# Spectral block on one core: three banks for the inverse column transform, a fifth layer 1 eviction on ScalarE, the second LN2 product behind layer 1

## Chip, cores and metric

The kernel runs on one core of a Trainium2 chip. The time is device time of one execution in microseconds (us), median of 3 executions; all data are float32.

## What is computed

Input x is (16, 56, 56, 64): 16 images of 56 x 56 pixels with 64 channels. Two layers follow each other.

```python
# layer 0: whitening over all pixels
f = x_flat - mean                                   # 64 x 50176
ff = (1 - EPS) * (f @ f.T) / (n - 1) + EPS * eye
f_hat = solve_triangular(cholesky(ff), eye) @ f     # then * gamma + beta
# layer 1: Fourier filter block and MLP, per image
h = layer_norm(x, n1_g, n1_b)
xf = rfft2(h)                                       # 56 x 29 frequencies, 8 blocks of 8 channels
o1 = relu(complex 8x8 products of xf with w1, + b1) # filter layer 1
o2 = softshrink(complex products of o1 with w2, + b2, 0.01)   # filter layer 2
h = irfft2(o2) + h + x
out = gelu(layer_norm(h, n2_g, n2_b) @ mw1 + mb1) @ mw2 + mb2 + h
```

## The kernel before

The 16 images go in 8 pairs; a pair is a tile of 112 rows (2 images x 56 image rows) and 56 x 64 columns. First comes the covariance of all pairs and its factorization (up to about 124 us), which gives the whitening matrix `wy`. Then the pairs run as a software pipeline written out by hand: each engine has its own instruction list, and they meet only at semaphores.

Step i (the `step` function of TensorE, ScalarE and VectorE) works on pair i, and besides on the pair before and the two after. TensorE does in order: `dft_h` (S1, transform along the columns, 8 chunks, line 1020), a whitening chunk of pair i+1 (line 1005), `dft_w` (S2, line 1030), a whitening chunk, `layer_1` (line 1045, four groups of two chunks), a whitening chunk, then seven slices of the MLP of pair i-1. Slice 0 begins with the transposes of `n2` (line 1106) and whitening chunks 3 to 6; slices 1 and 2 hold `layer_2` (line 1061), slices 3 and 4 `inv_w` (INVW, line 1072), slices 5 and 6 `inv_h` (FIN, line 1093, four pairs of chunks: the inverse column transform). In each slice come the MLP's two products (`mlp_in`, line 1115, and `mlp_out`, line 1124) and the transposes back (`turn_out`, line 1133). In slices 1 to 3 x of pair i+2 is transposed as well (line 990) for steps up to 5.

PSUM has eight banks. Bank 0 (`BANK_X`) takes x chunks and whitening chunks 0 to 4; banks 1 and 2 take the chunks of pair i from L2 on, in turn (`B_BANK`), and whitening chunks 5 and 6; bank 3 (`BANK_M`) the MLP's transposes and second product and its turned output; banks 4 to 7 the MLP's hidden values, and parts of S1, S2 and L1. A chunk's product waits until the chunk that had its bank before has been read; `free_b` and `free_c` issue that wait.

Evictions are split by kind. ScalarE reads S1, S2, INVW, the x chunks, `n2T` (line 1307), gelu (line 1314) and `mlp_t` (line 1323), and of the eight chunks of L1 those not in `L1_DVE` (line 1292, two instructions each). VectorE reads the others of L1 (line 680, two each), L2 (line 691, then a clamp from SBUF to SBUF, line 697), FIN (line 719), the whitening chunks (line 671) and the MLP's output slice (line 706). It also does the statistics (line 587) and the normalizations; `multiply_rstd` (line 632) is the product of LN2 for half of a pair. GpSimd does, for each pair, two long operations on the residual (`add_h`, lines 416 and 419), which wait for both products of the pair before (`n2_ready`), and then the difference that makes the softshrink, chunk by chunk (line 429), which gives `y_ready`. Chunk c of L2 has the buffer of chunk c-2, so VectorE's eviction waits for `y_ready` of that one. SyncE issues all transfers.

Of the kernel before, what the change touches and what calls it, by code (L numbers as in the profile page):

```python
# [35 lines left out]
PAIRS = B // 2  # L36
# [15 lines left out]
S1, S2, L1, L2, INVW, FIN, B_CHUNKS = 0, 8, 16, 24, 32, 40, 48  # L52
A_CHUNKS = 14
BANK_X, BANK_M, BANK_HID = 0, 3, 4
# [6 lines left out]
def last_pair(i):  # L61
    return i == PAIRS - 1


L1_DVE = (1, 3, 5, 7)
B_READERS = [("act",)] * B_CHUNKS
for _k in range(8):
    B_READERS[L2 + _k] = ("dve",)
    B_READERS[FIN + _k] = ("dve",)
for _k in L1_DVE:  # L70
    B_READERS[L1 + _k] = ("dve",)


def b_done(who, k):

    return sum(who in readers for readers in B_READERS[:k + 1])


B_ACT, B_DVE = (b_done(who, B_CHUNKS - 1) for who in ("act", "dve"))
# [23 lines left out]
B_BANK = [(1, 2, 4, 5, 6, 7)[k % 6] if k < L2 else 1 + k % 2 for k in range(B_CHUNKS)]  # L103
# [9 lines left out]

def fin_bank(i, k):

    return BANK_HID + k - 2 if i == 0 and 2 <= k < 6 else B_BANK[FIN + k]


def mlp_order(i):
# [55 lines left out]
def build(nc, x, consts, params, out):  # L175
# [5 lines left out]
    with ExitStack() as ctx:  # L181
# [3 lines left out]
        def sem(name):  # L185
            return ctx.enter_context(nc.semaphore(name))
# [7 lines left out]
        def pp(name, rows=128):  # L194
            return prm[0:rows, p_at[name][0]:p_at[name][1]]
# [84 lines left out]
        a_act, whitened = sem("a_act"), sem("whitened")  # L280
        b_act, b_dve = sem("b_act"), sem("b_dve")
# [10 lines left out]
        bank = [psum[:, j, :] for j in range(8)]  # L292
# [21 lines left out]
        def bc(ap2, n):  # L314

            return ap2.unsqueeze(2).broadcast_to((ROWS, n, C))
# [21 lines left out]
        with nc.Block() as block:  # L338
# [110 lines left out]
            def _(dve):  # L449
# [115 lines left out]
                def folded_weights():  # L565

                    dve.wait_ge(s_mlp_ps, 2)
                    nc.vector.tensor_tensor(hbias[:], hb_ps, pp("mb1"), ALU.add).then_inc(s_mlp, 1)
                    nc.vector.scalar_tensor_tensor(mw1s[:], mwm_ps, -float(ROWS) / C, mw1s[:], ALU.mult, ALU.add).then_inc(s_mlp, 1)
# [55 lines left out]
                def half_w(t, k):  # L625
                    return t[:, k * WP * C:(k + 1) * WP * C].rearrange("p (w c) -> p w c", c=C)

                def multiply_rstd(i, k):

                    if i == 0 and k == 0:  # L630
                        dve.wait_ge(r_begun, 3)
                    nc.vector.tensor_tensor(half_w(n2, k), half_w(rf[i % 2], k), bc(small[:, 8, k * WP:(k + 1) * WP], WP),  # L632
                                            ALU.mult).then_inc(n2_ready, 1)
# [24 lines left out]
                def ln2(i):  # L658
                    mean_rstd(i, 1)
                    if i < PAIRS - 2:  # L660
                        ev_whiten(i + 2, [0])
                    for k in range(2):
                        multiply_rstd(i, k)

                def ev_whiten(i, ks):
                    if i > 1:

                        dve.wait_ge(r_begun, 2 * i - 1)
                    for k in ks:
                        dve.wait_ge(pe_a, i * A_CHUNKS + 7 + k + 1)  # L670
                        nc.vector.tensor_tensor(  # L671
                            y_of(i)[:, k * 512:(k + 1) * 512].rearrange("p (w c) -> p w c", c=C),
                            bank[(WHITEN if i > 1 else SECOND_WHITEN)[k]][0:ROWS, :].rearrange("p (w c) -> p w c", c=C),
                            row("beta", 8), ALU.add).then_inc(whitened, 1)

                def ev_layer_1(i):
                    for k in L1_DVE:
                        dve.wait_ge(pe_b, i * B_CHUNKS + L1 + k + 1)
# [50 lines left out]
                def step(i, ahead, behind):  # L729
                    def slice_(s, e0, e1, e2, e3):  # L730

                        e0()
                        e1()
                        e2()
                        if behind and s > 0:
                            ev_mlp(i - 1, s - 1)
                        e3()

                    def next_(what, *args):
                        if ahead:  # L740
                            what(i + 1, *args)

                    def whitened_next(*ks):
                        if i > 0:
                            next_(ev_whiten, ks)
# [14 lines left out]
                    ev_layer_1(i)  # L760
                    if i == 0:
                        folded_weights()
                    slice_(0, lambda: whitened_next(2, 3, 4), lambda: whitened_next(5),
                           lambda: whitened_next(6), lambda: stats_next(0))
                    slice_(1, lambda: ev_layer_2(i, [0]), lambda: (ev_layer_2(i, [1]), stats_next(1)),
# [63 lines left out]
            def _(pe):  # L829
# [245 lines left out]

                def free_fin(i, k):

                    if i > 0 or k < 2:
                        return free_b(i, FIN + k)
                    if k >= 6:  # L1080
                        pe.wait_ge(b_dve, b_done("dve", FIN + k - 6))
                    return bank[fin_bank(i, k)]

                def inv_h(i, k):
# [163 lines left out]
            def _(act):  # L1248
# [38 lines left out]
                def ev_layer_1(i):  # L1287
                    for k in range(8):
                        if k not in L1_DVE:
                            act.wait_ge(pe_b, i * B_CHUNKS + L1 + k + 1)  # L1290
# [259 lines left out]
```

## Time and profile before

| | |
|---|---|
| median of 3 executions | 806.96 us (805.65 to 807.21) |
| the profiled execution | 809.76 us |
| its span | 808.0 us |
| busy: TensorE matmul, weight load | 765.6 us (95%), 531.2 us (66%) |
| busy: VectorE, ScalarE, GpSimd | 561.5 us (69%), 393.7 us (49%), 263.1 us (33%) |
| steps 2 to 5, each | 82.9 us |
| step 6, step 7 with what follows | 81.56 us, 122.75 us |

Busy shares are means over stages. The steps begin at 141.07 (step 0), 191.59, 272.19, 355.06, 437.94 (step 4), 520.82, 603.69 (step 6) and 685.25 us (step 7). Where the prediction reads a single step, it is step 4 unless it says otherwise. In the rows, line numbers are those of the kernel before; in brackets stands how long an engine was idle before the row and who released it.

### The profile page before, as it was taken

How to read it: one execution, taken by the hardware profiler on the slowest of the kernel's cores; microseconds unless marked ns; L12 is line 12 of the kernel's file. 1: busy time of each engine (PE TensorE's matmuls, PEld its weight loads, DVE VectorE, ACT ScalarE, POOL GpSimd, SP SyncE). 2: the span in 40 equal slices, each digit the busy share in tenths (PEclk: the TensorE clock that was granted, in tenths of full speed). 3: DMA queues.
4: the chain of work that ended last, by engine and by line, in shares of the span. 5: the costliest groups of instructions: out<-in, count | busy, mean ns of one | idle time of the engine just before them, and what ended most of it. 6: DMA issues, size and time to landing. Idle time of an engine off the chain costs nothing.

```text
span 808.0 us, 18673 instructions
## 1 busy us (share of the span) xinstructions
PE 765.6 (95%) x7561; PEld 531.2 (66%) x7561; DVE 561.5 (69%) x1860; ACT 393.7 (49%) x757; POOL 263.1 (33%) x107
## 2 busy tenths in 40 slices
PE   7998998998999999999999999999999999989887
PEld 5994558886666676657765777486748665747333
DVE  4568988799777677767685858585958695733651
ACT  0011006743756374736563656475646544755365
POOL 5000000953740364035412551245223622362000
PEclk9899999999999999999999999999999999999999
DMA  9934002011000210112010300130000000000012
GB/s 273 277 97 144 3 2 81 1 48 35 1 25 24 74 41 14 35 46 70 13 35 24 92 13 24 35 92 13 24 30 18 12 25 24 24 12 24 24 35 69
DMA packets 10375, 39.50 MB, mean 49 GB/s; under 512 B 1282, under 2 KB 1410, under 8 KB 8834
## 3 DMA queue, kind: packets, MB, share of 16 engines
q1 hardware_dynamic: 10290, 38.31, 16.4%
q8 instruction: 60, 0.98, 0.5%
q14 instruction: 25, 0.20, 0.1%
HBM read 25.46 MB, written 12.85 MB: 47 GB/s over the span
## 4 chain that ended last, share of the span: by engine, by line
PE 84%; DVE 12%; issue 2%; ACT 1%; DMA 0%; DVEq 0%; ACTq 0%
PE psum L1115 11%; PE psum L1124 11%; PE psum L1020 7%; PE psum L1061 7%; PE psum L1030 6%; PE psum L1072 6%; PE psum L1045 6%; PE psum L1093 5%; PE psum L1005 4%; PE psum L844 4%; PE psum L895 3%; PE psum L1133 3%; PE psum L990 3%; DVE stats L587 2%; PE psum L1106 2%
## 5 line engine op out<-in xcount | busy, mean ns | idle before, releaser
L1314 ACT ACTIVATE hid<-psum,hbias 128x448 f32<-128x448 f32 x224 | 123.8, 635 | 80.6 <-PE psum L1115 80.6
L411 POOL TENSOR_TENSOR rbuf<-ybuf,prm 112x2560 f32<-112x2560 f32 (+2 forms) x7 | 31.8, 4539 | 224.8 <-DVE hbuf L816 130.4
L1115 PE MATMUL psum<-n2T,mw1s 64*128 64x448 f32 x448 | 102.7, 576 | 1.7 <-ACT n2T L1307 1.7
L429 POOL TENSOR_TENSOR p_y<-layer,clamped 128x512 f32<-128x512 f32 x64 | 75.6, 1181 | 80.1 <-DVE clamped L697 80.1
L1124 PE MATMUL psum<-hid,prm 128*64 128x448 f32 x448 | 96.3, 552 | 1.9 <-DVE oslice L706 1.9
L691 DVE TENSOR_TENSOR layer<-psum,prm 128x512 f32<-128x512 f32 x64 | 40.3, 630 | 42.8 <-PE psum L1061 42.8
L1061 PEld LDWEIGHTS psum<-w2s,o_g 128*64 128x64 f32 x1856 | 60.1, 138 | 14.4 <-issue 8.9
L416 POOL TENSOR_TENSOR hbuf<-hbuf,prm 112x3584 f32<-112x3584 f32 x8 | 49.6, 6204 | 59.9 <-DVE n L632 59.9
L1072 PEld LDWEIGHTS psum<-cst,p_y 128*128 128x128 f32 x512 | 61.2, 192 | 10.6 <-issue 6.3
L1072 PE MATMUL psum<-cst,p_y 128*128 128x112 f32 x512 | 66.8, 277 | 0.5 <-DVE layer L691 0.5
L1061 PE MATMUL psum<-w2s,o_g 128*64 128x64 f32 x1856 | 66.1, 224 | 0.9 <-ACT o_g L1292 0.6
L1124 PEld LDWEIGHTS psum<-hid,prm 128*64 128x64 f32 x448 | 27.3, 136 | 58.4 <-issue 42.8
L1093 PE MATMUL psum<-u_r,cst 58*112 58x448 f32 x256 | 55.2, 551 | 8.3 <-DVE rbuf L719 4.1
L1115 PEld LDWEIGHTS psum<-n2T,mw1s 64*128 64x128 f32 x448 | 39.9, 189 | 30.0 <-issue 21.6
L1005 PE MATMUL psum<-wy,xT 128*112 128x128 f32 x448 | 57.1, 277 | 1.9 <-DVE ybuf L671 1.2
L1005 PEld LDWEIGHTS psum<-wy,xT 128*112 128x112 f32 x448 | 51.3, 177 | 10.9 <-issue 10.0
L1020 PEld LDWEIGHTS psum<-cst,hbuf 112*112 112x112 f32 x512 | 52.3, 177 | 9.2 <-issue 8.5
L1020 PE MATMUL psum<-cst,hbuf 112*112 112x116 f32 x512 | 55.1, 265 | 2.8 <-DVE rbuf L719 1.6
L1261 ACT COPY u_r<-psum 112x464 f32<-112x464 f32 x64 | 34.9, 545 | 45.7 <-PE psum L1020 45.7
L411 POOL TENSOR_TENSOR fbuf<-ybuf,prm 112x2560 f32<-112x2560 f32 (+1 forms) x6 | 24.4, 4075 | 93.8 <-DVE oslice L706 93.8
L1030 PE MATMUL psum<-cst,u_r 112*128 112x116 f32 x464 | 53.4, 276 | 1.3 <-ACT u_r L1261 1.3
L587 DVE BATCH_NORM_STATS2 stats<-ybuf 112x6 f32<-112x64 f32 x392 | 52.9, 207 | 1.8 <-ACT ybuf L1397 1.6
(135 smaller groups left out, 1382.3 us busy)
## 6 DMA issues: line engine op xcount, KB each, us to landing
xin<-x_dram SPq DMA_DIRECT2D x8, 1568.0 KB, 8.3
out_dram<-oslice SPq DMA_DIRECT2D x56, 224.0 KB, 2.2
ybuf<-x_dram SPq DMA_DIRECT2D x2, 1568.0 KB, 15.9
fbuf<-x_dram SPq DMA_DIRECT2D x2, 1568.0 KB, 19.1
xin<-x_dram SPq DMA_DIRECT2D x4, 392.0 KB, 4.9
n<-x_dram SPq DMA_DIRECT2D x1, 1568.0 KB, 21.3
n<-x_dram SPq DMA_DIRECT2D x4, 392.0 KB, 13.2
prm<-params_dram SPq DMA_DIRECT2D x1, 742.0 KB, 4.2
```

The source lines that it names most:

```text
L411: nc.gpsimd.tensor_tensor(r3, y3, row("b1", ws.stop - ws.start), ALU.add).then_inc(r_begun, 1)
L429: nc.gpsimd.tensor_tensor(yk, a, b, ALU.subtract).then_inc(y_ready, 1)
L587: last = nc.vector.bn_stats(stats[:, w, :], src[:, w * C:(w + 1) * C])
L1005: last = nc.tensor.matmul(t[0:ROWS, j * 128:(j + 1) * 128], xT[:, w * ROWS:(w + 1) * ROWS], wy[:], start=(i > 0), stop=True, skip_group_ch ...
L1020: last = nc.tensor.matmul(t[0:ROWS, j * 2 * KR:(j + 1) * 2 * KR], h_w[:, 4 * k + j, :], cc("f1", ROWS), start=True, stop=True)
L1030: last = nc.tensor.matmul(t[:, j * 4 * KF:(j + 1) * 4 * KF], u_r[0:ROWS, (4 * k + j) * 128:(4 * k + j + 1) * 128], cc("f2", ROWS), start=T ...
L1061: last = nc.tensor.matmul(t[C * r:C * r + C, j * C:j * C + C], o_g[:, at:at + C], w2s[:, 128 * half + C * r:128 * half + C * r + C], start ...
L1072: last = nc.tensor.matmul(t[:, j * 112:j * 112 + 112], y_v[:, 4 * k + j, :], cc("invw"), start=True, stop=True)
L1093: one = nc.tensor.matmul(t[d][0:ROWS, 0:7 * C], cc("invh")[rows, ROWS * m:ROWS * m + ROWS], g[rows], start=(m == 0), stop=(m == 1))
L1115: nc.tensor.matmul(t[:, 0:4 * ROWS], mw1s[C * v:C * v + C, HH * m:HH * m + HH], n2T[C * v:C * v + C, s % 2, :], start=True, stop=True).the ...
L1124: last = nc.tensor.matmul(t[C * v:C * v + C, 0:4 * ROWS], pp("mw2")[:, C * m:C * m + C], hid[:, s % 2, m, v, :], start=(m == 0), stop=(m = ...
L1314: nc.scalar.activation(hid[:, s % 2, m, v, :], bank[CH_MLP[i].bank[k]][:, 0:4 * ROWS], ACT.Gelu, bias=hbias[:, m:m + 1]).then_inc(c_act, 1)
```

## The change

Three edits. In steps 1 to 6 the chunks of the inverse column transform take banks 1, 2 and 0 in turn instead of 1 and 2, so that a chunk waits for the one three before it; chunk 2, the first in bank 0, waits for the last x chunk's eviction (for the last whitening chunk's in step 6). Chunk 1 of L1 goes from VectorE to ScalarE in all eight steps, which then has 0, 1, 2, 4 and 6. And VectorE does the second product of LN2 after its evictions of L1 instead of right after the first.

```diff
-L1_DVE = (1, 3, 5, 7)
+L1_DVE = (3, 5, 7)
...
 def fin_bank(i, k):
 
-    return BANK_HID + k - 2 if i == 0 and 2 <= k < 6 else B_BANK[FIN + k]
+    if i == 0 and 2 <= k < 6:
+        return BANK_HID + k - 2
+    return (1, 2, BANK_X)[k % 3] if 0 < i < PAIRS - 1 else B_BANK[FIN + k]
...
                     if i < PAIRS - 2:
                         ev_whiten(i + 2, [0])
-                    for k in range(2):
-                        multiply_rstd(i, k)
+                    multiply_rstd(i, 0)
...
                     ev_layer_1(i)
                     if i == 0:
                         folded_weights()
+                    if behind:
+                        multiply_rstd(i - 1, 1)
                     slice_(0, lambda: whitened_next(2, 3, 4), lambda: whitened_next(5),
...
                 def free_fin(i, k):
 
-                    if i > 0 or k < 2:
+                    if k < 2 or last_pair(i):
                         return free_b(i, FIN + k)
-                    if k >= 6:
-                        pe.wait_ge(b_dve, b_done("dve", FIN + k - 6))
+                    if i == 0:
+                        if k >= 6:
+                            pe.wait_ge(b_dve, b_done("dve", FIN + k - 6))
+                        return bank[fin_bank(i, k)]
+                    if k == 2 and i < PAIRS - 2:
+                        pe.wait_ge(a_act, (i + 3) * 7)
+                    elif k == 2:
+                        pe.wait_ge(whitened, (i + 2) * 7)
+                    else:
+                        pe.wait_ge(b_dve, i * B_DVE + b_done("dve", FIN + k - 3))
                     return bank[fin_bank(i, k)]
```

VectorE around layer 1 of step 1, before (`n` is the buffer `n2`, the output of the LN2 product; `o_g` the output of layer 1):

```order
L632 TENSOR_TENSOR n<-rbuf,small 112x1792 [waits r_begun]
L632 TENSOR_TENSOR n<-rbuf,small 112x1792
L671 TENSOR_TENSOR ybuf<-psum,prm 112x512 [waits pe_a,r_begun]
L680 TENSOR_SCALAR o_g<-psum,prm 64x15x29 [waits pe_b]
L680 TENSOR_SCALAR o_g<-psum,prm 64x15x29
L680 TENSOR_SCALAR o_g<-psum,prm 64x15x29 [waits pe_b]
L680 TENSOR_SCALAR o_g<-psum,prm 64x15x29
L680 TENSOR_SCALAR o_g<-psum,prm 64x14x29 [waits pe_b]
L680 TENSOR_SCALAR o_g<-psum,prm 64x14x29
L680 TENSOR_SCALAR o_g<-psum,prm 64x14x29 [waits pe_b]
L680 TENSOR_SCALAR o_g<-psum,prm 64x14x29
L671 TENSOR_TENSOR ybuf<-psum,prm 112x512 [waits pe_a,r_begun]
```

The same place with the change (lines 634, 672 and 681 are the former 632, 671 and 680):

```order
L634 TENSOR_TENSOR n<-rbuf,small 112x1792 [waits r_begun]
L672 TENSOR_TENSOR ybuf<-psum,prm 112x512 [waits pe_a,r_begun]
L681 TENSOR_SCALAR o_g<-psum,prm 64x15x29 [waits pe_b]
L681 TENSOR_SCALAR o_g<-psum,prm 64x15x29
L681 TENSOR_SCALAR o_g<-psum,prm 64x14x29 [waits pe_b]
L681 TENSOR_SCALAR o_g<-psum,prm 64x14x29
L681 TENSOR_SCALAR o_g<-psum,prm 64x14x29 [waits pe_b]
L681 TENSOR_SCALAR o_g<-psum,prm 64x14x29
L634 TENSOR_TENSOR n<-rbuf,small 112x1792
L672 TENSOR_TENSOR ybuf<-psum,prm 112x512 [waits pe_a,r_begun]
```

One eviction of two instructions has left the queue, and the second product now stands behind the rest of them and ahead of the whitening chunks 2 to 6.

TensorE at the inverse column transform of step 1, before (`u_r` holds the spectrum that `inv_h` reads):

```order
L1093 MATMUL psum<-u_r,cst 112x448 [waits b_act]
L1093 MATMUL psum<-u_r,cst 112x448 x3
L1106 MATMUL psum<-cst,n 128x112 [waits c_act]
L1106 MATMUL psum<-cst,n 128x112 x3
L1093 MATMUL psum<-u_r,cst 112x448 [waits b_dve,b_act]
L1093 MATMUL psum<-u_r,cst 112x448 x3
```

And with the change:

```order
L1104 MATMUL psum<-u_r,cst 112x448 [waits b_act]
L1104 MATMUL psum<-u_r,cst 112x448 x3
L1117 MATMUL psum<-cst,n 128x112 [waits c_act]
L1117 MATMUL psum<-cst,n 128x112 x3
L1104 MATMUL psum<-u_r,cst 112x448 [waits b_dve,a_act,b_act]
L1104 MATMUL psum<-u_r,cst 112x448 x3
```

The order is the same; the second pair of chunks waits in addition for the x chunks' evictions (`a_act`), and `b_dve` there stands for one eviction fewer.

## Rows read from the trace of the kernel before

**Rows 1.** Page, part 4: the chain that ended last, shares of the span

```profile
PE 84%; DVE 12%; issue 2%; ACT 1%; DMA 0%; DVEq 0%; ACTq 0%
```

**Rows 2.** Stretches: length, busy PE, PEld, DVE, ACT, POOL, PEclk, DMA, GB/s

```profile
437.94:520.82 82.88, 81.18 (x735) 56.45 (x735) 59.38 (x195) 47.39 (x91) 31.66 (x12) 1.00 0.14 40
707.40:710.00 2.60, 0.59 (x5) 0.41 (x5) 1.27 (x2) 1.69 (x3) 2.46 (x2) 1.00 0.00 0
710.00:713.40 3.40, 3.40 (x9) 1.43 (x9) 0.00 (x0) 1.19 (x3) 3.40 (x1) 0.50 0.00 0
```

**Rows 3.** Waits of PE in step 4: total us, times, longest

```profile
PE psum L1093 <- DVE rbuf L719: 0.9, 1, 0.9
```

**Rows 4.** Timeline, PE behind layer 1 of step 4: start us, duration us

```profile
454.97 5.92 PE L1045 MATMUL psum<-p_y,w1s 64*128 64x435 f32 x32
...
462.36 0.57 PE L1106 MATMUL psum<-cst,n 112*128 112x112 f32 x4 [0.41 <-ACT o_g L1292]
463.13 1.10 PE L1005 MATMUL psum<-wy,xT 128*112 128x128 f32 x8 [0.19 <-DVE ybuf L671]
464.15 1.77 PE L1115 MATMUL psum<-n2T,mw1s 64*128 64x448 f32 x8
```

**Rows 5.** Timeline, inverse column transform of step 4, VectorE and PE

```profile
509.82 1.15 DVE L719 TENSOR_TENSOR rbuf<-psum,rbuf 112x448 f32<-112x448 f32 x2 [3.37 <-PE psum L1093]
...
511.12 1.76 PE L1093 MATMUL psum<-u_r,cst 58*112 58x448 f32 x8 [0.87 <-DVE rbuf L719]
```

**Rows 6.** Timeline, ScalarE at layer 1 of step 4

```profile
456.73 1.27 ACT L1292 ACTIVATE o_g<-psum,prm 64x435 f32<-64x435 f32 x2 [1.56 <-PE psum L1045]
458.19 3.95 ACT L1292 ACTIVATE o_g<-psum,prm 64x435 f32<-64x435 f32 x6 [0.19 <-PE psum L1045]
```

**Rows 7.** Timeline, VectorE around layer 1 of step 4

```profile
450.98 3.95 DVE L632 TENSOR_TENSOR n<-fbuf,small 112x1792 f32<-112x1792 f32 x2
...
456.77 5.49 DVE L680 TENSOR_SCALAR o_g<-psum,prm 64x435 f32<-64x435 f32 x8 [0.94 <-PE psum L1045]
462.29 0.69 DVE L671 TENSOR_TENSOR ybuf<-psum,prm 112x512 f32<-112x512 f32 x1
```

**Rows 8.** Timeline, GpSimd's two long operations in step 4

```profile
455.01 6.20 POOL L416 TENSOR_TENSOR hbuf<-hbuf,prm 112x3584 f32<-112x3584 f32 x1 [8.22 <-DVE n L632]
461.35 7.94 POOL L419 TENSOR_TENSOR rbuf<-rbuf,hbuf 112x3584 f32<-112x3584 f32 x1
```

**Rows 9.** Timeline, a clamp beside GpSimd in step 0

```profile
166.43 1.29 POOL L429 TENSOR_TENSOR p_y<-layer,clamped 128x512 f32<-128x512 f32 x1 [0.36 <-DVE clamped L697]
...
166.98 1.01 DVE L697 TENSOR_SCALAR clamped<-layer 128x512 f32<-128x512 f32 x1
```

**Rows 10.** Timeline, layer 2 in slice 1 of step 4, VectorE and PE

```profile
474.18 0.43 DVE L697 TENSOR_SCALAR clamped<-layer 128x512 f32<-128x512 f32 x1
...
476.17 0.97 DVE L587 BATCH_NORM_STATS2 stats<-ybuf 112x6 f32<-112x64 f32 x7
...
478.11 0.68 DVE L706 TENSOR_TENSOR oslice<-psum,fbuf 112x512 f32<-112x512 f32 x1
...
479.98 1.72 PE L1124 MATMUL psum<-hid,prm 128*64 128x448 f32 x8
...
482.68 0.69 DVE L691 TENSOR_TENSOR layer<-psum,prm 128x512 f32<-128x512 f32 x1 [2.06 <-PE psum L1061]
```

**Rows 11.** Timeline, step 6: the long add and the second MLP product

```profile
627.09 7.96 POOL L419 TENSOR_TENSOR rbuf<-rbuf,hbuf 112x3584 f32<-112x3584 f32 x1
...
644.65 1.72 PE L1124 MATMUL psum<-hid,prm 128*64 128x448 f32 x8
```

**Rows 12.** Timeline, step 7: layer 1's last evictions and two MLP products

```profile
706.71 1.98 DVE L680 TENSOR_SCALAR o_g<-psum,prm 64x406 f32<-64x406 f32 x3
...
709.99 3.43 PE L1115 MATMUL psum<-n2T,mw1s 64*128 64x448 f32 x8 [0.62 <-ACT n2T L1307]
...
724.86 1.72 PE L1124 MATMUL psum<-hid,prm 128*64 128x448 f32 x8
```

## The prediction

> **What bounds the kernel now.** I read the chain of waits first, then the stretches, then TensorE's waits, then the timelines around the three edited places. The chain runs through TensorE for most of the span [rows 1]. A step of the steady part, step 4 (437.94 to 520.82), keeps TensorE busy for 81.18 of 82.88 us, with VectorE at 59.38, ScalarE at 47.39 and GpSimd at 31.66 [rows 2]. So what counts is where TensorE stands still. The largest hole of a step is 0.87 us [rows 3], ahead of the second pair of products of the inverse column transform. The other two the change touches are 0.41 and 0.19 us behind filter layer 1, before the transposes of slice 0 and before whitening chunk 3 [rows 4]. Each us taken from a hole is a us of time, and so is each us added; the work itself leaves no slack.
>
> **Part 1, three banks for the inverse column transform.** Call its eight chunks F0 to F7, two per product pair. Before, the second pair waits for F0 and F1 to be evicted. Afterwards it waits for F0 and for ScalarE's last x chunk, evicted two slices earlier, so that wait is met. The two evictions take 1.15 us together, from 509.82 to 510.97, and TensorE starts at 511.12 [rows 5]. One eviction less is 0.57 us earlier, and the transposes ahead are over by then (511.12 less 0.87 is 510.25). Pairs three and four now wait one eviction less too, but had no hole; the next column transform still waits for F6. Bounds: 0, and the whole 0.87. I take -0.57 in steps 1 to 6, **-3.4 us**. Step 7 keeps its old banks.
>
> **Part 2, ScalarE takes a fifth eviction of layer 1.** The first chunk of the first pair is evicted in 1.27 us, the other three follow in 3.95 from 458.19 to 462.14, with gaps of 0.19 at most [rows 6]. Five in a row make 456.73 + 5 x 1.26 = 463.0, so ScalarE is done 0.9 us later. VectorE has three instead of four, but the last one is bound by supply: layer 1's products end at 454.97 + 5.92 = 460.89 [rows 4], and one eviction is 5.49 / 4 = 1.37, which gives 462.26, just where it ends now [rows 7]. Taking one away early in the queue buys nothing at its end. TensorE waits for both engines before the slice 0 transposes. In step 0, which has no second product, this is **+0.9 us**; in steps 1 to 6 it lies beneath part 3, and in step 7 too.
>
> **Part 3, the second product of LN2 behind layer 1.** The two products take 3.95 us, 1.98 each, and end at 454.93 [rows 7]. The place that the second one leaves had room: VectorE then only adds one whitening chunk and is idle for 0.94 us before its first eviction of layer 1 at 456.77. The new place is not. Queued behind the product on VectorE is the eviction of whitening chunk 2, and since chunks 0 to 4 share one bank, TensorE's chunk 3 waits for it: 462.29 + 0.69 gives 462.98, TensorE starts at 463.13. Now the product runs from 462.27 to 464.25, the eviction to 464.94, chunk 3 starts at 465.1: **+2.0 us per step** up to here. Bounds: nothing if the product ended by 462.3, 2.0 if all of it lies there; the rows put all of it there.
>
> GpSimd is the second one behind it. Its two long operations on the residual wait for both products. They began at 455.01, right behind 454.93, and ended at 461.35 + 7.94 = 469.29 [rows 8]. They will begin at 464.33, that is 9.3 us later, and end at 478.6. Before, the first chunk of layer 2 was clamped at 474.18 [rows 10], 4.9 us after the long add had ended; shifted by 2.0 it comes at 476.2, while the add still runs.
>
> What happens then is shown on a small scale. In step 0 a clamp was issued at 166.98, while GpSimd ran from 166.43 to 167.72; it took 1.01 instead of 0.43 us and ended at 167.99, 0.27 after GpSimd [rows 9]. So the clamp stands until GpSimd's instruction is over. Taken for the long add, the clamp of chunk 0 ends at 478.6 + 0.27 = 478.9. The Trainium skill says the same as a rule (SBUF — State Buffer, "SBUF: two separate sides"): VectorE in a 2-port mode and GpSimd take an exclusive lock for a whole instruction, and the loser blocks. By that rule the sum is the one below; if only short instructions hold it up, as the row alone shows, it is that of rival B.
>
> From there, with the durations of [rows 9, 10] (GpSimd's short ones 1.28, an eviction 0.69, each starting some 0.05 before the one ahead has ended): GpSimd's first short one 479.0 to 480.25; the eviction of chunk 1 ends at 479.5, its clamp stands until 480.5; statistics 0.97, to 481.4; eviction of chunk 2, to 482.0; clamp, to 482.4; then the output slice (VectorE line 706), 0.68, to 483.1. TensorE's second MLP product (line 1124) needs that slice's bank. It started at 479.98 and would by the 2.0 start at 482.0; now it starts at 483.2. So **+3.2 in place of +2.0**. Behind it VectorE had an idle stretch of 2.06 us before the next slice, so both are in step again.
>
> **The sum.** Steps 1 to 5: 3.2 - 0.57 = 2.65 each, 13.2. Step 6 has no x chunks between its layer 2 products, so it reaches that place sooner: its long add ended at 635.05, now at 644.35; the clamp ends at 644.6, the same 4.3 us as in step 4 (478.9 to 483.2) follow, and the product of 644.65 starts at 648.95 [rows 11]. That is +4.3 - 0.57 = +3.7. Step 7: layer 1 is evicted at 708.69, the product ends at 710.7; the two long operations (6.20, 0.14 between them, and 7.94) end at 725.0, and the clamp of chunk 0, due long before, at 725.3. Then two short ones each hold a clamp (2 x 1.63: 0.08 to start, 1.28, 0.27), the output slice and the start follow: 729.3 against 724.86, **+4.4** [rows 8, 12]. With step 0's 0.9: 0.9 + 13.2 + 3.7 + 4.4 = **+22.2 us**. The profiled execution took 809.76, 2.80 above the median of 806.96; the same sum on it gives 832.0, on the median **829.2**.
>
> **Rivals.**
> A, the sum above: 829.2.
> A with the clock. In step 7 TensorE did only four transposes between 707.4 and 710.0, and the granted clock then fell from 1.00 to 0.50 (2.4 to 1.2 GHz) for 3.4 us [rows 2]: the products of the MLP's input took 3.43 us [rows 12] instead of 1.77 [rows 4], 1.66 more. With the change TensorE does only four transposes between 461.95 and 465.1 in every step. The fall would bring it to 483.7 instead of 483.2, so most is hidden by VectorE: +0.5 in five steps; and in step 7 a new hole of 3.3 us could bring a full 1.66. Together up to 833.4. The Trainium skill (TensorE: Matmul & The Clock Gate, "Part 4: PE-mode transpose") has transposes not counting as busy the way products do; that would make this the rule in all seven steps, with the time just given.
> B, the clamps aren't held by the long add. Then the first short one still waits for its end and chunk 2 for the short one, but in steps 1 to 5 TensorE isn't held again: 5 x (2.0 - 0.57) = 7.1; step 6: 644.35 + 1.36 (start and short one) + 1.78 (eviction, clamp, output slice) + 0.15 = 647.65, +3.0 - 0.57 = 2.4; step 7 the same way 728.3, +3.4; step 0 0.9. Sum 13.8: 820.8. Against it speaks the clamp of [rows 9], which waited to the end of what ran beside it.
> C, the banks bring nothing because TensorE waits for another release there: 829.2 + 3.4 = 832.6. Against it: the list of waits names VectorE alone.
> D, faster. If VectorE finished its three evictions 2.0 us sooner than its four, by 460.3, the product would be over at 462.3, the whitening would not wait, the transposes would wait only for ScalarE, and the bank's 3.4 us would stand against little: 803.6. Against it stands the end of layer 1's products at 460.89, which comes before the last eviction can start.
>
> **The numbers.** A measurement of this kernel can tell about 0.2%, 1.6 us, from no change. A 0.70, A with the clock 0.08, B 0.12, C 0.04, D 0.03, and 0.03 for a mix of small effects that ends within 0.2%. Slower by more than 0.2%: 0.94; within: 0.03; faster: 0.03. The range must take in B and the top of the clock case, with a little for the extrapolated lock: 819 to 834. That leaves out D and the mix.
>
> **What would show it.** Right: TensorE's hole before the second inverse pair falls from 0.87 to 0.3; the hole before the slice 0 transposes grows to 1.3 and that before whitening chunk 3 to 1.4; a new hole of 1.2 before line 1124's second product (4 or so in step 7, part of it already before a layer 2 product), released by the output slice; the clamps of chunk 0 take about 2.7 us in steps 1 to 5; GpSimd's long operations start about 9.3 us later; a steady step lasts 85.5 us. Wrong: clamps of 0.43 beside the long add (B), or a hole before whitening chunk 3 that stayed at 0.2 (D).

## The result and the profile after

| | before | after |
|---|---|---|
| median | 807.09 us (4 runs, 805.65 to 809.62) | 835.19 us (4 runs, 834.34 to 837.45) |
| ratio | | 1.0349, 95% interval 1.0316 to 1.0382 |
| the profiled execution, its span | 809.76, 808.0 us | 835.47, 833.7 us |
| busy: TensorE matmul, VectorE, ScalarE, GpSimd | 765.6, 561.5, 393.7, 263.1 us | 776.4, 564.2, 403.7, 263.4 us |

28 us slower. The forecast was 829.2 with a range up to 834, so the sign was right and the size fell 1.2 us outside. Lines 691, 697, 706 and 1124 of before are 692, 698, 707 and 1135 here; 1005, 1106, 1115, 1061 and 1093 are 1008, 1117, 1126, 1064 and 1104; 632, 671, 416, 419 and 429 are 634, 672, 418, 421 and 431.

The chain of waits of the changed kernel, shares of the span, answers to [rows 1]:

```profile
PE 80%; DVE 14%; issue 3%; ACT 2%; DMA 0%; DVEq 0%; ACTq 0%
```

TensorE gives four points to VectorE, issue and ScalarE. The stretches of the changed kernel, a line for each step from 1 to 6 and one for step 7 with the rest (columns as in [rows 2]), and under them the stretches behind layer 1 in steps 1, 2 and 4 and one in step 7:

```profile
192.51:276.00 83.49, 79.24 (x722) 55.45 (x723) 61.43 (x205) 49.30 (x93) 33.41 (x13) 1.00 0.05 15
276.00:362.20 86.20, 83.03 (x735) 56.96 (x735) 59.31 (x193) 48.76 (x93) 31.72 (x12) 0.98 0.13 38
362.20:448.37 86.17, 83.01 (x734) 57.58 (x735) 59.31 (x193) 48.64 (x93) 31.69 (x12) 0.98 0.13 39
448.37:535.79 87.42, 84.25 (x735) 58.11 (x735) 58.13 (x193) 48.76 (x93) 31.71 (x12) 0.96 0.13 38
535.79:621.98 86.19, 83.03 (x735) 57.28 (x735) 59.30 (x193) 48.71 (x93) 31.66 (x12) 0.98 0.13 39
621.98:707.51 85.53, 79.64 (x707) 54.64 (x707) 59.50 (x193) 44.45 (x86) 31.71 (x12) 0.98 0.07 20
707.51:833.70 126.19, 108.50 (x830) 63.99 (x830) 63.46 (x191) 68.05 (x129) 25.97 (x11) 0.97 0.10 30
...
219.20:222.60 3.40, 3.40 (x29) 2.57 (x26) 1.08 (x3) 2.21 (x4) 3.40 (x1) 1.00 0.00 0
304.30:307.70 3.40, 3.40 (x10) 1.19 (x8) 0.69 (x1) 1.16 (x2) 3.40 (x1) 0.50 0.00 0
...
475.00:481.90 6.90, 6.14 (x21) 3.81 (x22) 1.31 (x2) 1.96 (x4) 6.76 (x2) 0.51 0.00 0
...
748.00:751.40 3.40, 2.97 (x26) 2.04 (x28) 3.33 (x5) 0.00 (x0) 2.68 (x3) 0.50 0.00 0
```

Against the steps of before, the differences are +0.79 (step 0), +2.89, +3.33, +3.30, +4.54, +3.32 (steps 1 to 5), +3.97 (step 6) and +3.44 us (step 7 with the rest), with 0.13 at the start: 25.7, the difference of the two spans. A reader should see a second thing: the granted clock was 1.00 in all of step 4 before [rows 2] (and in its steps 1 to 6) and is 0.96 to 0.98 in steps 2 to 6. Behind layer 1 of step 1 it stayed at 1.00; at the same place of steps 2 to 6 it fell to 0.50 (the lower of the two levels, 1.2 GHz).

VectorE, TensorE and GpSimd in step 1 of the changed kernel, where the clock did not fall, from three timelines (start us, duration us). Answers to [rows 4, 8, 10]:

```profile
216.83 6.21 POOL L418 TENSOR_TENSOR hbuf<-hbuf,prm 112x3584 f32<-112x3584 f32 x1 [20.16 <-DVE n L634]
223.18 7.99 POOL L421 TENSOR_TENSOR fbuf<-fbuf,hbuf 112x3584 f32<-112x3584 f32 x1
231.53 1.29 POOL L431 TENSOR_TENSOR p_y<-layer,clamped 128x512 f32<-128x512 f32 x1 [0.36 <-DVE clamped L698]
```

```profile
227.95 0.69 DVE L692 TENSOR_TENSOR layer<-psum,prm 128x512 f32<-128x512 f32 x1 [2.52 <-PE psum L1064]
228.67 2.77 DVE L698 TENSOR_SCALAR clamped<-layer 128x512 f32<-128x512 f32 x1
...
232.08 1.01 DVE L698 TENSOR_SCALAR clamped<-layer 128x512 f32<-128x512 f32 x1
```

```profile
215.41 0.60 PE L1117 MATMUL psum<-cst,n 112*128 112x112 f32 x4 [1.00 <-ACT o_g L1303]
217.62 1.10 PE L1008 MATMUL psum<-wy,xT 128*112 128x128 f32 x8 [1.60 <-DVE ybuf L672]
...
235.69 1.72 PE L1135 MATMUL psum<-hid,prm 128*64 128x448 f32 x8 [1.09 <-DVE oslice L707]
```

The long add ends at 223.18 + 7.99 = 231.17, and the clamp that needs 0.43 us alone ends at 231.44, 0.27 later. The wait shows nowhere as idle time: VectorE counts as busy for 2.77 us. TensorE's three holes are 1.00, 1.60 and 1.09: the first ahead of the transposes, the second ahead of whitening chunk 3, the third ahead of the MLP's second product.

The timeline of the changed kernel in step 4, the same place (about 256 us later), where the clock did fall:

```profile
473.55 0.60 PE L1117 MATMUL psum<-cst,n 112*128 112x112 f32 x4 [0.99 <-ACT o_g L1303]
...
475.76 2.02 PE L1008 MATMUL psum<-wy,xT 128*112 128x128 f32 x8 [1.61 <-DVE ybuf L672]
...
477.71 3.36 PE L1126 MATMUL psum<-n2T,mw1s 64*128 64x448 f32 x8
...
481.31 7.98 POOL L421 TENSOR_TENSOR rbuf<-rbuf,hbuf 112x3584 f32<-112x3584 f32 x1
...
489.68 0.43 DVE L698 TENSOR_SCALAR clamped<-layer 128x512 f32<-128x512 f32 x1
```

The whitening chunk takes 2.02 instead of 1.10 us and the MLP's first products 3.36 instead of 1.77. TensorE comes to layer 2 so late that the clamp starts after the add has ended at 489.29, and takes its 0.43 us; the hole before line 1135 is gone. In steps 2, 3, 5 and 6 the clamp took 1.12 to 1.32 us, the rest of an add that was nearly over. So the clamp of 2.77 us stands in step 1 alone of the steps from 1 to 6.

Step 7 of the changed kernel, VectorE and TensorE, answers to [rows 12]:

```profile
739.57 7.93 POOL L421 TENSOR_TENSOR fbuf<-fbuf,hbuf 112x3584 f32<-112x3584 f32 x1
...
741.89 5.89 DVE L698 TENSOR_SCALAR clamped<-layer 128x512 f32<-128x512 f32 x1
...
748.43 1.34 PE L1064 MATMUL psum<-w2s,o_g 128*64 128x64 f32 x20 [4.19 <-DVE layer L692]
...
752.24 0.97 PE L1135 MATMUL psum<-hid,prm 128*64 128x448 f32 x4
```

A clamp of 0.43 us stands for 5.89 and ends at 747.78, 0.28 after the add (747.50).

### The profile page after: what moved, and what is told of

It is laid out like the page before. It is cut to its first block, busy times and chain, and to the rows that moved or that the text cites. A ratio compares the mean times of both kernels' runs of the same rounds, so it can differ in the third digit from the quotient of the medians.

```text
span 833.7 us, 18673 instructions
## 1 busy us (share of the span) xinstructions
PE 776.4 (93%) x7561; PEld 537.0 (64%) x7561; DVE 564.2 (68%) x1844; ACT 403.7 (48%) x773; POOL 263.4 (32%) x107
## 4 chain that ended last, share of the span: by engine, by line
PE 80%; DVE 14%; issue 3%; ACT 2%; DMA 0%; DVEq 0%; ACTq 0%
PE psum L1126 11%; PE psum L1135 10%; PE psum L1023 6%; PE psum L1033 6%; PE psum L1075 6%; PE psum L1064 6%; PE psum L1104 5%; PE psum L1048 5%; PE psum L1008 5%; PE psum L847 4%; PE psum L898 3%; PE psum L1144 3%; DVE stats L589 2%; PE psum L993 2%; PE psum L1117 2%
## 5 line engine op out<-in xcount | busy, mean ns | idle before, releaser
L1126 PE MATMUL psum<-n2T,mw1s 64*128 64x448 f32 x448 | 107.0, 599 | 2.0 <-ACT n2T L1318 2.0
L1008 PE MATMUL psum<-wy,xT 128*112 128x128 f32 x448 | 61.0, 289 | 10.4 <-DVE ybuf L672 9.7
L1008 PEld LDWEIGHTS psum<-wy,xT 128*112 128x112 f32 x448 | 54.7, 187 | 20.9 <-issue 20.0
L1126 PEld LDWEIGHTS psum<-n2T,mw1s 64*128 64x128 f32 x448 | 41.9, 201 | 33.0 <-issue 25.0
L672 DVE TENSOR_TENSOR ybuf<-psum,prm 112x512 f32<-112x512 f32 x42 | 29.0, 691 | 46.9 <-PE psum L1008 46.5
L1303 ACT ACTIVATE o_g<-psum,prm 64x435 f32<-64x435 f32 (+1 forms) x80 | 49.4, 617 | 12.0 <-PE psum L1048 10.7
```

The costliest lines, as they stand in the source:

```text
L1008: last = nc.tensor.matmul(t[0:ROWS, j * 128:(j + 1) * 128], xT[:, w * ROWS:(w + 1) * ROWS], wy[:], start=(i > 0), stop=True, skip_group_ch ...
L1126: nc.tensor.matmul(t[:, 0:4 * ROWS], mw1s[C * v:C * v + C, HH * m:HH * m + HH], n2T[C * v:C * v + C, s % 2, :], start=True, stop=True).the ...
L1303: last = nc.scalar.activation(dst, src, ACT.Relu, bias=bias)
```

## The experiments

The theory was the sum of the prediction (banks -0.57 a step, product +2.0, held clamp +1.2). Its rivals were that the clock causes the loss and that GpSimd's lateness costs nothing by itself. Ratios are against the kernel before on the same chip: 808.39 us (12 runs) for e1 to e4, 808.11 (22) for e5 to e8, 808.19 (7) for e9 and e10. A ratio of 0.001 is 0.8 us. Kernels of different groups are compared by their ratios.

**e1, the banks alone** (the kernel before with the change's `fin_bank` and `free_fin`).

```diff
-    return BANK_HID + k - 2 if i == 0 and 2 <= k < 6 else B_BANK[FIN + k]
+    if i == 0 and 2 <= k < 6:
+        return BANK_HID + k - 2
+    return (1, 2, BANK_X)[k % 3] if 0 < i < PAIRS - 1 else B_BANK[FIN + k]
```

> The kernel before with the three banks alone. Theory (stall and clock): the hole before the second inverse pair falls from 0.87 to 0.34 us in steps 1 to 6, nothing else moves: 6 x 0.53 = 3.2 us less, a ratio of 0.996. Rival (the other parts pay only because the banks shift the work): no change, 1.000.

Measured: 804.36 us, ratio 0.9951 (0.9935 to 0.9967), -4.0 us. The waits of TensorE in a steady step (columns as in [rows 3]; the inverse transform is line 1103 here):

```profile
PE psum L1116 <- ACT o_g L1302: 0.4, 1, 0.4
PE psum L1103 <- DVE rbuf L721: 0.3, 1, 0.3
```

The hole went from 0.87 to 0.34 and the steady steps from 82.88 to 82.35. This part of the change is a gain.

**e2, ScalarE's fifth eviction alone.**

```diff
-L1_DVE = (1, 3, 5, 7)
+L1_DVE = (3, 5, 7)
```

> The kernel before with ScalarE's fifth eviction alone. Theory: the hole before the slice 0 transposes grows from 0.41 to about 1.0, and whitening chunk 3 starts about 0.5 later; +0.8 in step 0, +0.5 in steps 1 to 6, +0.6 in step 7, no more falls of the granted clock in steps 2 to 6: +4 us, 1.005. Rival (the clock falls because of the longer wait for ScalarE): falls in steps 2 to 6 here too, +12 us or more, 1.015.

Measured: 812.58 us, 1.0053 (1.0038 to 1.0069), +4.2 us. TensorE behind layer 1 of step 4 in its timeline:

```profile
464.23 0.60 PE L1106 MATMUL psum<-cst,n 112*128 112x112 f32 x4 [1.00 <-ACT o_g L1292]
464.67 1.04 PE L1005 MATMUL psum<-wy,xT 128*112 128x128 f32 x8
```

The hole before the transposes grew from 0.41 to 1.00, that before the whitening chunk (0.19) closed, and a step took 83.25, +0.37. The clock stayed at 1.00 in steps 1 to 6: a hole of 1.0 and four transposes alone did not bring it down. One more thing moved: layer 1's products ended 23.12 us into the step instead of 22.94. Chunk 7 of layer 1 has the bank of chunk 1, whose eviction now ends 21.35 us into the step on ScalarE instead of 20.19 on VectorE, and the last pair of chunks starts at 21.50 instead of 21.42.

**e3, the product alone.**

```diff
-                    for k in range(2):
-                        multiply_rstd(i, k)
+                    multiply_rstd(i, 0)
...
+                    if behind:
+                        multiply_rstd(i - 1, 1)
```

> The kernel before with the second LN2 product moved alone. Theory: holes of 0.4 and about 2.2 us behind layer 1, the clock falls there in most steps, GpSimd 9 us later, clamp of chunk 0 held up to the end of the long add: about 3.8 us a step in steps 1 to 6 and 3 to 4 in step 7, +24 to +27 us, 1.030 to 1.034. Rival (the product and the fifth eviction share the loss): +15 us, 1.019.

Measured: 839.36 us, 1.0387 (1.0365 to 1.0409), +31 us, more than the theory's share. Steps 3 and 4 of its stretches:

```profile
366.43:452.99 86.56, 82.81 (x734) 57.39 (x735) 60.63 (x195) 47.38 (x91) 31.64 (x12) 0.98 0.13 39
452.99:540.76 87.77, 84.01 (x734) 58.08 (x735) 59.50 (x195) 47.50 (x91) 31.72 (x12) 0.96 0.13 38
```

+3.7 and +4.9 against 82.88, with the clock below 1.00 in steps 1 to 5 (for 6.8 us in steps 2 and 4, for 3.4 in the others). In step 6, where it did not fall, the clamp took 2.78 us. The moved product holds the whole loss; the other two parts together take some 3 us off it.

**e4, the clock held up.** The changed kernel with idle products on TensorE, whose results nobody reads, three before the transposes of slice 0 and five behind them.

```diff
+                    if behind:
+                        pe.wait_ge(b_dve, i * B_DVE + b_done("dve", L1 + 3))
+                        fill_hole(3, 2)
...
+                        if ahead:
+                            fill_hole(5, 4)
```

> The changed kernel with dummy products (results never read) in the two holes behind layer 1: three ahead of the slice 0 transposes and five behind them, some 0.27 us each, so that TensorE is busy there without being later. Theory (the falls of the clock come from these holes and cost time): granted clock 1.00 in steps 2 to 6, the clamp of chunk 0 then takes about 2.8 us as in step 1, steps 1 to 5 last 85.5 or less and the whole 3 to 5 us less than the changed kernel: 830 to 832. Rival (GpSimd's long add bounds the step anyway, the fall is hidden by it): time within 1 us of the changed kernel although the clock stays up.

Measured: 834.01 us, 1.033 (1.0308 to 1.0351). Step 4 in its stretches, and the one long wait of TensorE in step 3 (line 1140 is the MLP's second product):

```profile
447.88:533.64 85.76, 83.55 (x750) 58.12 (x751) 60.95 (x193) 48.64 (x93) 31.73 (x12) 1.00 0.14 39
```

```profile
PE psum L1140 <- DVE oslice L707: 1.1, 1, 1.1
```

Steps 1 to 6 ran at 1.00 and each clamp of chunk 0 took 2.76 to 2.78 us. By the ratios the kernel is 1.5 us below the changed one, which the two intervals can't tell from nothing. The traces tell more. Steps 2 to 5 took 2.9 us less than in the changed kernel. The span gained only 1.5 (832.2 against 833.7), since in this execution the clock fell at two other places: in step 0 at 163.93, where nothing was added (1.0 us longer), and in step 7 at 802.23, behind the transposes that wait for the last LN2 product (step 7 with the rest took 127.26 against 126.19); the start was 0.7 shorter. So the clock behind layer 1 is worth 2.9 of the 28 us. Where it falls there, TensorE is late by most of what it would have waited for VectorE: a step with one fall of 3.4 us takes 0.43 us more than one with none (86.19 against 85.76), and step 4, where it lasted for 6.8, 1.65 more.

**e5, the long add in four instructions.**

```diff
-                    nc.gpsimd.tensor_tensor(r4[i % 2], r4[i % 2], h_tok, ALU.add).then_inc(r_ready, 1)
+                    for q in range(4):
+                        ws = slice(q * W // 4, (q + 1) * W // 4)
+                        last = nc.gpsimd.tensor_tensor(r4[i % 2][:, ws], r4[i % 2][:, ws], h_tok[:, ws], ALU.add)
+                    last.then_inc(r_ready, 1)
```

> The changed kernel with GpSimd's long add cut into four instructions of a quarter each (about 2.1 us), one signal behind the last. Theory (a clamp stands until the instruction beside it is over): the clamp of chunk 0 stands for the rest of one quarter, at most 2.5 us in step 7 instead of 5.89 and 1.5 or less in step 1 instead of 2.77; the holes before the second MLP product in step 1 (1.08) and before layer 2 in step 7 (4.19) shrink or go. In steps 2 to 6 the clock still falls and TensorE is late anyway, so in all only 2 to 4 us less than the changed kernel: 831 to 833. Rival (the clamp waits for all of the add, however it is cut): clamps of 2.77 and 5.89 as before, no change.

Measured: 838.2 us, 1.0379 (1.0338 to 1.042), no gain; its six executions lie between 832.98 and 841.55. Step 3, in which the clock did not fall, and VectorE and GpSimd in it, timelines:

```profile
361.05:446.49 85.44, 81.45 (x735) 56.44 (x735) 60.29 (x193) 48.71 (x93) 32.37 (x15) 1.00 0.14 39
```

```profile
399.50 1.09 DVE L701 TENSOR_SCALAR clamped<-layer 128x512 f32<-128x512 f32 x1
400.51 0.68 DVE L695 TENSOR_TENSOR layer<-psum,prm 128x512 f32<-128x512 f32 x1
401.22 1.66 DVE L701 TENSOR_SCALAR clamped<-layer 128x512 f32<-128x512 f32 x1
404.12 0.69 DVE L695 TENSOR_TENSOR layer<-psum,prm 128x512 f32<-128x512 f32 x1 [0.35 <-POOL p_y L434]
```

```profile
394.00 8.60 POOL L423 TENSOR_TENSOR fbuf<-fbuf,hbuf 112x896 f32<-112x896 f32 x4
402.54 2.71 POOL L434 TENSOR_TENSOR p_y<-layer,clamped 128x512 f32<-128x512 f32 x2
```

The clamp now waits for a quarter (1.09 us), so it is held by the instruction that runs, not by the add as a whole. It changes little: GpSimd ends its add at 402.60 (0.6 later than in one piece, 8.60 against 7.98), and the eviction of chunk 2 needs the buffer that GpSimd's next operation frees. VectorE waits there instead. In the profiled execution the clock fell in steps 4, 5 and 6 only, though TensorE's two holes behind layer 1 are 1.00 and 1.61 us in every step from 1 to 6. Where it did not fall, the cut is worth 0.3 us a step (85.44, against 85.76 in e4 with the add whole); where it fell once, the step takes 86.21, as in the changed kernel. And step 7 is 2.2 us longer than there (128.4 against 126.2).

**e6, both: idle products and the add in four** (the two diffs above).

> Both at once, the dummy products of e4 and the cut add of e5. Theory (fall of the clock and held clamp hide each other, so that each alone gives little): with both gone only the moved product's 2.0 us less the banks' 0.53 are left, steps 1 to 5 last 84.3 to 84.7 us, and the whole comes to 822 to 825, more below the changed kernel than e4 and e5 are together. Rival (a third cost is behind most of the loss): 829 or more.

Measured: 831.75 us, 1.0298 (1.0271 to 1.0324), by the ratios 4.1 us below the changed kernel, where 10 to 13 were expected. Its steps 2 to 5 take 85.44 to 85.47 at a clock of 1.00. Waits of TensorE in step 4, and a stretch of step 7:

```profile
PE psum L1143 <- DVE oslice L710: 0.8, 1, 0.8
PE psum L1016 <- DVE ybuf L675: 0.4, 1, 0.4
```

```profile
743.90:750.70 6.80, 5.20 (x50) 3.16 (x52) 2.61 (x6) 0.63 (x1) 2.81 (x3) 0.50 0.12 36
```

The hole before the MLP's second product stays at 0.8 us, with neither the clock nor the long hold. What keeps it open is GpSimd's late end, of which 0.6 us comes with the cut. The expectation had left out both that cost and the wait of chunk 2 for GpSimd. In step 7, where no idle products were added, the hole there is 3.77 us in one piece, and the clock fell right at it for 6.8 us; step 7 with the rest took 128.2 us against 126.2 in the changed kernel. So steps 1 to 6 gained 4.8 us and step 7 gave 2.0 of them back.

**e9, lateness without the work.** e3 with the moved product covering 1 of its 28 columns; the other 27 of the second half are left out for pairs 0 to 6. GpSimd starts as late as it must behind layer 1, VectorE has hardly any work there. The third argument is the number of columns.

```diff
-                        multiply_rstd(i - 1, 1)
+                        multiply_rstd(i - 1, 1, 1)
```

> As e3 (the product moved alone), but the moved product covers one of its 28 columns; the other 27 of the second half are left out in pairs 0 to 6. It takes some 0.2 us instead of 2.0, at the same place, so GpSimd still begins some 7.3 us later than in the kernel before. Theory (besides the 2.0 us on VectorE, GpSimd's lateness costs by itself): whitening chunk 3 only 0.2 later, no fall of the clock in steps 1 to 6, GpSimd's long add ends some 1.5 to 2 us after the clamp of chunk 0 is due, and a hole of about 1 us before the second MLP product; steps 1 to 5 last 83.8 to 84.2 us, step 7 some 2 to 3 us more, the whole 8 to 11 us above before, 1.010 to 1.014. Rival (only the 2.0 us on VectorE count): before plus 1.5 us at most, 1.002.

Measured: 820.75 us, 1.0153 (1.0137 to 1.017), +12.6 us. A steady step, and the waits of TensorE in it:

```profile
441.66:526.00 84.34, 81.31 (x734) 56.44 (x735) 60.51 (x195) 47.47 (x91) 31.65 (x12) 1.00 0.14 40
```

```profile
PE psum L1125 <- DVE oslice L705: 1.1, 1, 1.1
...
PE psum L1006 <- DVE ybuf L670: 0.5, 1, 0.5
```

The clock stays at 1.00, the clamps take 2.78 us in every step from 1 to 6, and a step is 1.46 longer than before. Of these, 0.25 are the small product's own delay ahead of whitening chunk 3 (25.44 us into step 4 against 25.19), and 1.2 come at the MLP's second product, behind the held clamp. That is the price of GpSimd's start behind layer 1, with hardly any work moved: some 11 of the 12.6 us (12.6 less 6 x 0.25), though that engine is busy for only a third of the span. The clock can't be the cause in steps 1 to 6, since it did not fall there. The 11 us are no fixed share of e3's 31, where the clamp itself comes later.

**e10, GpSimd waits for the first product only** (changed kernel; its addition reads nothing that the second product writes).

```diff
-                    pool.wait_ge(n2_ready, 2 * i)
+                    pool.wait_ge(n2_ready, 2 * i - 1)
```

> The changed kernel, but GpSimd's two long operations wait for the first product alone, so they begin about 9 us sooner and run beside the moved one, which shares no data with them. Theory (an operation of VectorE with two SBUF inputs can't run beside a GpSimd instruction either): the moved product, issued while the first or second long operation runs, stands until that one is over, 5 us or more instead of 2.0, whitening chunk 3 comes that much later, and the whole is slower than the changed kernel by 15 us or more. Rival (only the clamp is held, since it alone takes the fast mode): the product takes 2.0 us, the clamps 0.43, and the whole is 5 us or more faster than the changed kernel.

Measured: 863.34 us, 1.068 (1.0662 to 1.0698), by the ratios 27 us slower than the changed kernel. Timelines of step 3 in it:

```profile
394.53 7.88 POOL L421 TENSOR_TENSOR fbuf<-fbuf,hbuf 112x3584 f32<-112x3584 f32 x1
```

```profile
397.54 6.76 DVE L634 TENSOR_TENSOR n<-rbuf,small 112x1792 f32<-112x1792 f32 x1
```

```profile
405.17 2.02 PE L1008 MATMUL psum<-wy,xT 128*112 128x128 f32 x8 [6.34 <-DVE ybuf L672]
```

The add ends at 402.41, the product at 404.30, 1.89 later, about its own 2.02: it did next to nothing until GpSimd had finished. So the wait for both products, which looks needless, keeps GpSimd off VectorE. A step takes 92.2 us. The clock has a share in that: it fell in the hole of 6.34 us (7.01 in step 1) and stayed at 0.50 for 10.2 us in each of steps 1 to 6. How large the share is, no run here tells. Keeping GpSimd early with the product late does not help.

**e7 and e8, the useful part extended.** e7 is e1 with three banks in step 7 too (and the waits of `free_fin` to match).

```diff
+    if i == PAIRS - 1:
+        return (1, 2, BANK_X, 1, 2, 1, 2, 1)[k]
```

> The kernel before with three banks, in step 7 too. Theory: the hole of 0.87 before the second inverse pair falls to 0.34 in step 7 as well, 0.5 us less than e1: 803.9 if before is at 808.4. Rival (step 7 goes on bound by VectorE's statistics): as e1.

Measured: 803.5 us, 0.9949 (0.9932 to 0.9966; 12 runs). The intervals can't tell it from e1 (0.9951). e8 adds idle products to step 7 (4 and 2 around the transposes of slice 0, 8 before those of slice 3 in the last MLP) to hold the clock there.

```diff
+                    if last_pair(i):
+                        pe.wait_ge(b_dve, i * B_DVE + b_done("dve", L1 + 3))
+                        fill_hole(4, 2)
...
+                        if s == 1:
+                            fill_hole(8, 1)
```

> e7 with dummy products in the holes of step 7 behind layer 1 and ahead of the transposes that wait for the last LN2 product, the places where the granted clock falls in the kernel before (710.0 and 778.3). Theory: no fall there, up to 1.7 us less for each, 2 to 3 in all against e7, ratio to before 0.991 to 0.993. Rival (these falls are hidden by ScalarE and VectorE, as most of those of the changed kernel were): as e7 within 1 us.

Measured: 803.23 us, 0.9948 (0.9924 to 0.9971), by the ratios the same as e7. The stretch from 700 to 780 of e8, its step 7 with the rest, and that of e7:

```profile
700.00:780.00 80.00, 74.61 (x628) 43.33 (x626) 41.40 (x127) 44.23 (x81) 21.52 (x10) 1.00 0.08 24
681.47:800.74 119.27, 108.96 (x858) 65.62 (x858) 59.31 (x193) 66.90 (x127) 25.98 (x11) 0.99 0.11 32
```

```profile
682.26:803.34 121.08, 108.59 (x830) 63.55 (x830) 59.28 (x193) 67.12 (x127) 25.93 (x11) 0.97 0.10 32
```

The clock was held, and in the profiled executions step 7 is 1.8 us shorter: 1.1 us are gained by the start of the second inverse pair (66.60 us into the step against 67.71), where e7's clock had fallen behind layer 1, and the rest in the last 5 us. The medians show 0.3, and their intervals, some 2 us to either side, can't tell 1.8 from nothing. Whether these idle products gain stays open.

## Where the prediction was right, and where it was wrong

**Right: what bounds the kernel, and the sign.** In step 1, where the clock stayed up, each added us of hole was a us of time: 3.42 us at the MLP's second product, less 0.53 from the banks, are its 2.89. From step 2 on the slower clock took up the third hole.

**Right: part 1.** -0.57 a step was forecast, e1 gave -0.53; the hole closed to 0.34 (0.3 forecast). It had to be run alone, since in the changed kernel it is under the losses.

**Part 2, right in step 0, a little short in the others.** +0.9 in step 0, measured +0.79. That ScalarE's lateness would lie beneath part 3 held in the main: e3 (+3.87%) and e1 (-0.49%) make 3.38%, and the changed kernel has 3.49%, well within the intervals. But the sum took the end of layer 1's products as fixed. With the fifth eviction on ScalarE they end 0.18 us later (e2, and the changed kernel), and whitening chunk 3 then starts 27.39 us into a steady step instead of e3's 27.24. So part 2 costs some 0.15 us in each of steps 1 to 6, where the sum had nothing.

**Right, a little small: part 3.** TensorE's whitening chunk 3 starts 2.21 us later within step 1 (217.62 - 192.51 = 25.11, against 214.49 - 191.59 = 22.90), where 2.0 was forecast; the MLP's second product 3.42 later (43.18 against 39.76), where 3.2 was. Most of the missing 0.2 is part 2's, the end of layer 1's products, 20.85 against 20.66 us into the step; in e3 chunk 3 comes 2.05 later. GpSimd's start, 9.3 us later by the forecast, is 9.5 later in step 4 (26.60 us into it against 17.07). The clamp took 2.77 as forecast (2.7), but in step 1 only and not in steps 1 to 5: with the clock down, TensorE came later and met less of the add. The first two holes are 1.0 and 1.6 us where 1.3 and 1.4 were forecast.

**Right in mechanism, wrong in size: step 7.** The clamp ends 40.27 us into the step, 40.05 was forecast. To the second product it is +5.12 (44.73 against 39.61) for the forecast's +4.4; the clock was at 0.50 from 748.0. But what follows took 81.46 instead of 83.14 us. This 1.7 us is a fall of the clock too, in the kernel before. From the transposes that wait for the last LN2 product to the last wait of TensorE, before and after:

```profile
777.44:803.93 26.49, 25.61 (x128) 11.05 (x129) 4.15 (x6) 16.74 (x30) 0.00 (x0) 0.94 0.15 45
```

```profile
804.82:829.66 24.84, 23.96 (x129) 10.45 (x129) 4.15 (x6) 16.64 (x30) 0.00 (x0) 1.00 0.16 48
```

In the profiled execution of before the clock fell at 778.26 for 3.4 us, just behind these transposes. In the changed kernel it fell at 795.79, ahead of them, where TensorE waits for VectorE anyway: the hole there is then 1.11 us instead of 2.36, and the transposes start as long after those ahead of them (8.87 us) either way. The stretch takes 26.45 to 26.49 us in e3 and e4 too, where the clock fell behind the transposes, and 24.84 or 24.85 in all other runs. e1, e2 and e9, whose code is that of before at this place, are among these: the 1.65 us belong to the execution, not to the change.

**Wrong: the clock's term in the sum, the chance it was given, and the base.** The step that failed is the one that took the sum without the clock as the likeliest (0.70 against 0.08) and so put the clock's term in steps 2 to 5 at nothing; it measured 2.9 us. The row that spoke for it was there, four transposes with holes and a fall to 0.50 in step 7 [rows 2], and the fall came in five of the six steady steps. Its price was about right where it came once (0.43 us, 0.5 forecast), and short in step 4, where it lasted twice as long (1.65). In step 6 it cost nothing that can be seen: 3.97 against e4's 3.96 (85.52) with the clock held. Two smaller terms failed beside it: part 2 in steps 1 to 6, and a difference read from one execution, set on the median and bounded only by the rivals. The account, by the two spans:

| | forecast | measured |
|---|---|---|
| step 0 | +0.9 | +0.79 |
| steps 1 to 5 without the clock, 5 x 2.65 | +13.2 | +14.4 (5 x 2.89) |
| the clock in steps 2 to 5 | 0 | +2.9 (0.44, 0.41, 1.65, 0.43) |
| step 6 | +3.7 | +3.97 |
| step 7 to the second product | +4.4 | +5.12 |
| the rest (-1.65 of it the late fall in before), and the start | 0 | -1.55 |
| sum | +22.2 | +25.7 |

The other 2.4 us between 25.7 and the 28.1 of the medians is the profiled execution of before, 2.7 above the median of its runs, against one of after that is at its median. The late fall of the clock would be 1.65 of these 2.7 if the other executions of before did not have it; they have no trace, so that is not shown. The range should have been wider by what one execution differs from another.

**Rival B, which the runs bring near but not about.** It had 1.2 us a step less than the sum if the clamps were free of the long add. The clamps of the changed kernel were not free (2.77 us, 5.89 in step 7). With the add cut in four (e6) a step gained only 0.29 (85.47 against 85.76). The account of the rest is put together from the rows of e5 and e6, and no run separates its parts: the cut makes GpSimd end 0.6 later, and that end is on the path, since chunk 2 needs the buffer that GpSimd frees behind it; and the clamp of chunk 2 then takes 0.68 instead of 0.43 beside GpSimd's next operation. 0.3 + 0.6 + 0.25 is the 1.1 us of the hole.

**Open.** Why the clock fell behind layer 1 in steps 2 to 6 but not in step 1, and in e3 in steps 1 to 5 but not in 6, with the same instructions, no run here tells. In e5, with the same two holes (1.0 and 1.6 us), it fell in steps 4 to 6 only, so the two holes alone do not settle it; and the four executions of the changed kernel had a mean granted clock of 0.973 twice and 0.968 twice. e2 and e9 show that a hole of 1.0 with the transposes, or two of 0.4, did not bring it down in any steady step.

## What to carry to other kernels

An operation moved behind a block of evictions moves the engine that waits for it by the length of that block; follow that engine to its next deadline, however low its busy share is, since its lateness alone made some 11 us here. On VectorE and GpSimd a collision shows as a long duration of a short operation and not as idle time, so compare long instances of a line with its shortest before believing "busy". Test a change of three edits one by one: here one edit was a gain of 0.5% hidden under another's loss of 3.9%. And where one profiled execution is the base of a sum, look where its clock fell: one fall of 3.4 us cost nothing ahead of a wait and 1.65 us behind it.

## What the runs showed of the hardware

- A clamp of 128x512 (0.43 us alone) issued beside a GpSimd operation ended 0.27 to 0.28 us after it (changed kernel, steps 1 and 7), whether 2.5 us or 5.6 us of that were left, and after a quarter when the operation was cut in four. Evictions from PSUM beside the same add kept their 0.68 us.
- A product of VectorE with both inputs in SBUF (2.02 us) took 6.76 beside GpSimd's add and ended 1.89 us after it (e10).
- Cutting GpSimd's add of 112x3584 in four made it 8.60 instead of 7.98 us (e5, step 3), and 8.42 in steps 4 to 6 of e5, where no clamp ran between two quarters.
- Products at the lower clock level took 3.36 instead of 1.77 us, yet the five falls of steps 2 to 6 cost about 2.9 us in all, since TensorE would have waited for VectorE in most of that time.
- A fall of the clock for 3.4 us late in step 7 made the stretch from the last LN2 product's transposes on 26.49 instead of 24.84 us where it came behind them (before, e3, e4), and left it at 24.84 or 24.85 where it came ahead of them or not at all (the other runs).
